# One transformer megakernel: the expert layer in steps of two units, a changed fill table, x2 transposes ahead of the bias product

## The chip, the cores and the metric

One core of a Trainium2 chip runs the whole program in one launch. The metric is the device time of that core in microseconds (us), as the median of several executions. Engines: PE is TensorE, DVE is VectorE, ACT is ScalarE, POOL is GpSimd, SP is SyncE (it only issues transfers).

## The reference

Sixteen images and sixteen texts of 128 tokens become sequences of 178 tokens of width 192 (49 image tokens, one class token, the text). Two layers follow. The first is an attention with a masked diagonal. The second is an attention whose logits are z-scored, followed by a layer of four experts of which each token takes two:

```python
h = concat([tokenize(x), txt])
h = h + attention(layernorm(h))                  # 12 heads, the token itself masked out
s = layernorm(h)
logits = gamma * zscore(Q K^T / 4);  a = softmax(logits) V Wo
x2 = layernorm(s + a)
combine = top2(softmax(x2 Wg + bg))              # 4 experts
hid = relu(x2 W1[e] + b1[e])                     # 192 -> 768
y   = hid W2[e] + b2[e]                          # 768 -> 192
h = h + layernorm(x2 + sum_e combine[e] * y[e])
```

## The kernel before

The sixteen sequences are taken in eight pairs. After the tokenizer (until about 166 us) the kernel runs nine rounds, each with up to three pairs in flight: pair a in the first attention, pair b in the second, pair m in the expert layer. `rounds` writes them out: round 0 (a=0), round 1 (a=1, b=0), rounds 2 to 6 (a, b=a-1, m=a-2, and the front of pair a+1), round 7 (a=7, b=6, m=5, no next pair), round 8 (b=7, m=6, no a), and a last round with m=7 alone. Rounds 2 to 6 and the last use the table `FILL`, round 7 `FILL_A7`, round 8 `FILL_B7`.

A round on PE: the gate products of pair b of the round before (L977), then for pair b turning its rows into columns (`pe_turn_in`, L747), query and key projections (L755), value projection (L763), the four products of the z-score (`pe_deviation`, L876 to L899); for pair a the max pass (`pe_max_pass`: logits whose row maximum DVE takes, L790 and L796, DVE L1271), the rows of maxima (L823), the exp pass (logits again, ACT's exp at L1031, the product with the values at L849); then max pass and rows for b; the output of a (`pe_out`: L858, L864, L763), the exp pass of b, the output of b; then turning in, query and key of the next pair (L747, L755); then what is left of the expert layer (`moe.rest()`), the transposes of x2 of pair b (L964), and the value projection of the next pair. The gate products of b wait for DVE's `x2T_lo` (L1389).

The expert layer of pair m is 24 units (4 experts, six blocks of 128 hidden columns). Unit u has a first product F(u), 5 matmuls of 370 columns (L644), ACT's relu into one of two `hid` buffers (L679), and a second product S(u), 3 matmuls that the profile shows as 6 instructions (L666). After each sixth S, DVE adds the expert's share to `acc` (`expert`, L694). At the end comb is transposed (call it C, L635), ACT copies it (L683), PE multiplies it with the bias b2 (`bias`, B, L654), and DVE adds that (L703, L705).

These units are cut into 50 steps, and every engine takes its part of the same steps at the same named points of its own program. The table says how many steps stand at each point:

```python
def point(self, name, u=None):
    self.steps(self.fill[name] if u is None else self.fill[name][u])
```

Step 2u is F(u); step 2u+1 is S(u-1); step 48 is C and S(23); step 49 is B. The order is fixed by the program, and each engine runs its own in order; waits between engines are semaphores. The steps on DVE matter for the order there: the share of an expert stands at the point in which its sixth S falls. DVE's order around a round's end is: output of b, the chain that makes x2 (to L1378), the scaling for the next pair b (L1135), the point "next query", the splits of the next pair's queries and keys into three bf16 terms (`splits`, L1142 to L1145, eight operations), `moe.rest()`, then `x2T_lo`.

## Time and profile before

| | |
|---|---|
| three executions | 1286.83, 1287.30, 1294.15 us (median 1287.3) |
| profiled execution | 1291.78 us |
| its span, first to last instruction | 1290.0 us |
| mean granted TensorE clock | 0.884 of 2.4 GHz |
| busy | PE 1095.4 us (85%), PE weight loads 802.2, DVE 682.1 (53%), ACT 399.7 (31%), POOL 54.1 |

The profiled execution is 1.8 us longer than its span and 4.5 us above the median. By round it runs from 391 to 512 us (round 2), about 119.6 us each for rounds 3 to 6, to 1110 (round 7), to 1225 (round 8), and to 1290 (the last).

### The profile page before, as it was taken

To read this page: it belongs to the slowest core of one execution; us is meant where nothing else is said; L and a number is where in the kernel's file an instruction comes from. 1 tells how busy PE (TensorE), PEld (TensorE's weight loads), DVE (VectorE), ACT (ScalarE), POOL (GpSimd) and SP (SyncE) were. 2 spreads that over 40 slices of the span, in tenths; PEclk is the share of its full clock that TensorE was granted. 3 is DMA by queue.
4 is the path that set the end of the run, shared out by engine and by line. 5 is a ranking of instruction groups with operands and counts; after the bars stand their busy time and mean duration, and the time that the engine had idled before them with its cause. 6 is when DMAs were issued, how large, how long until landed. Compare 5 with 4: busy or idle time off the path is not lost.

```text
span 1290.0 us, 18666 instructions
## 1 busy us (share of the span) xinstructions
PE 1095.4 (85%) x7404; PEld 802.2 (62%) x7404; DVE 682.1 (53%) x1874; ACT 399.7 (31%) x905; POOL 54.1 (4%) x89
## 2 busy tenths in 40 slices
PE   7898645587779999999999999999999999985896
PEld 4343323354448668857776786678578667773795
DVE  1467685345454466654763674655557652632332
ACT  1222221212232433334323434333343234221321
POOL 6011100000000000000000000000000000000000
PEclk9898855755779989989998999899999989895988
DMA  8000051053005202320422043014204220022000
GB/s 296 0 1 0 16 152 26 7 97 61 11 7 119 49 8 56 78 43 9 84 51 44 8 105 66 13 34 100 44 8 82 51 43 2 1 64 29 1 10 8
DMA packets 38478, 60.74 MB, mean 47 GB/s; under 512 B 5060, under 2 KB 30264, under 8 KB 38072
## 3 DMA queue, kind: packets, MB, share of 16 engines
q1 hardware_dynamic: 36112, 56.84, 20.5%
q10 hardware_dynamic: 2280, 2.72, 0.7%
q8 instruction: 58, 0.95, 0.3%
q14 instruction: 28, 0.23, 0.1%
HBM read 42.76 MB, written 16.34 MB: 46 GB/s over the span
## 4 chain that ended last, share of the span: by engine, by line
PE 63%; DVE 13%; ACT 4%; issue 3%; DMA 3%; SPq 1%; POOL 0%; DVEq 0%; ACTq 0%; POOLq 0%
PE PS L666 14%; PE PS L644 11%; PE PS L755 7%; DVE mx L1271 6%; PE PS L849 5%; PE PS L763 5%; PE PS L790 5%; PE PS L796 3%; PE PS L805 2%; PE PS L858 2%; DMA qst<-mrows 1%; PE PS L887 1%; PE PS L977 1%; ACT probs L1031 1%; SPq L1471 1%
## 5 line engine op out<-in xcount | busy, mean ns | idle before, releaser
L666 PE MATMUL PS<-w,hid 128*128 128x192 f32 x1152 | 232.1, 339 | 3.0 <-DVE acc L694 1.8
L679 ACT ACTIVATE hid<-PS,b 128x370 f32<-128x370 f32 x192 | 109.1, 569 | 331.6 <-PE PS L644 329.8
L666 PEld LDWEIGHTS PS<-w,hid 128*128 128x128 f32 x1152 | 199.0, 197 | 12.8 <-issue 4.7
L1271 DVE TENSOR_REDUCE mx<-PS 128x2 f32<-128x356 f32 x288 | 129.8, 522 | 131.6 <-PE PS L790 103.5
L1031 ACT ACTIVATE probs<-PS 128x356 f32<-128x356 f32 x288 | 112.9, 484 | 35.6 <-PE PS L790 20.6
L790 PE MATMUL PS<-kst,qst 96*128 96x178 bf16 x384 | 71.5, 284 | 31.7 <-DMA kst<-scr_k 13.6
L644 PE MATMUL PS<-x2T_hi,w_hi 128*128 128x370 f32 x192 | 91.7, 478 | 0.0
L755 PE MATMUL PS<-xT,w_at 96*96 96x370 f32 x192 | 76.0, 546 | 8.9 <-ACT q L998 5.2
L805 PE MATMUL PS<-masks,ident_bf 128*128 128x256 bf16 (+1 forms) x288 | 79.9, 278 | 0.0
L790 PE MATMUL PS<-qst,kst 99*128 99x178 bf16 x384 | 58.0, 254 | 21.7 <-DMA qst<-mrows 17.5
L849 PE MATMUL PS<-probs,va 128*17 128x178 f32 x1536 | 70.8, 327 | 6.4 <-ACT probs L1031 6.4
L790 PEld LDWEIGHTS PS<-kst,qst 96*128 96x128 bf16 x384 | 27.2, 106 | 66.0 <-DVE mx L1271 30.7
L1292 DVE RECIPROCAL rs<-PS 128x36 f32<-128x36 f32 x16 | 6.1, 383 | 114.4 <-PE PS L858 114.4
L644 PE MATMUL PS<-x2T_hi,w_lo 128*128 128x370 f32 x192 | 66.2, 345 | 0.0
L644 PE MATMUL PS<-x2T_lo,w_hi 128*128 128x370 f32 x192 | 66.1, 344 | 0.0
L644 PE MATMUL PS<-x2T_hi,w_rest 128*128 128x370 f32 x192 | 66.1, 344 | 0.0
L644 PE MATMUL PS<-x2T_lo,w_rest 128*128 128x370 f32 x192 | 65.6, 342 | 0.0
L755 PEld LDWEIGHTS PS<-xT,w_at 96*96 96x96 f32 x192 | 33.4, 182 | 41.9 <-ACT q L998 8.9
L790 PEld LDWEIGHTS PS<-qst,kst 99*128 99x128 bf16 x384 | 28.7, 101 | 46.9 <-issue 30.8
L849 PEld LDWEIGHTS PS<-probs,va 128*17 128x17 f32 x1536 | 41.0, 99 | 24.4 <-ACT probs L1031 9.3
L694 DVE SCALAR_TENSOR_TENSOR acc<-PS,comb,acc 128x192 f32<-128x192 f32 x72 | 25.5, 410 | 54.3 <-PE PS L666 54.2
L377 DVE SCALAR_TENSOR_TENSOR dwo<-pad_l,chan,dwo 96x441 f32<-96x441 f32 x48 | 38.0, 793 | 27.9 <-ACT cw L301 26.4
(222 smaller groups left out, 1724.4 us busy)
## 6 DMA issues: line engine op xcount, KB each, us to landing
qst<-scr_q SPq DMA_DIRECT2D x96, 144.0 KB, 4.8
scr_q<-qs SPq DMA_DIRECT2D x16, 432.0 KB, 3.3
scr_k<-ks SPq DMA_DIRECT2D x16, 432.0 KB, 4.7
kst<-scr_k SPq DMA_DIRECT2D x16, 432.0 KB, 5.0
kst<-scr_k SPq DMA_DIRECT2D x16, 288.0 KB, 5.9
cols<-in_x_cols SPq DMA_DIRECT2D x6, 392.0 KB, 8.2
w<-in_w SPq DMA_DIRECT2D x1, 2304.0 KB, 25.2
kst<-scr_k SPq DMA_DIRECT2D x16, 144.0 KB, 6.3
```

What stands on the lines that cost most here:

```text
L377: ch.link(nc.vector.scalar_tensor_tensor(out=out, in0=image_rows(PAD_OF[r][:, 0, :], tap_offset(t), n), scalar=col(C_DW + 18 * r + t), in1 ...
L644: ins = nc.tensor.matmul(PS[:, 4 + u % 2, 0:XN], w[:, f], x[:, plane, 0:XN], start=(k == 0), stop=(k == 4))
L666: ins = nc.tensor.matmul(tile_psum((6, 7), i), hid[u % 2][:, 128 * i:128 * i + 128], w2[:, u, :], start=(j == 0 and i != 1), stop=(j == FT ...
L679: nc.scalar.activation(hid[u % 2][:, 0:XN], PS[:, 4 + u % 2, 0:XN], ACT.Relu, bias=b1[:, u:u + 1]).then_inc(S["h_ready"], 1)
L755: ins = nc.tensor.matmul(PS[0:HC, FRONT[s][m], 0:XN], w_at[:, w, k, HC * m:HC * m + HC], x[:, k, 0:XN], start=(k == 0), stop=(k == 1))
L763: ins = nc.tensor.matmul(tile_psum(banks, i), tile_cols(x, k, i), w_at[:, w, k, :], start=(k == 0), stop=(k == 1))
L790: ins = nc.tensor.matmul(PS[:, bank, T * b:T * b + T], still[0:rows_, h, TP * b:TP * b + NTXT], move[0:rows_, h, TP * b:TP * b + T], start ...
L796: ins = nc.tensor.matmul(PS[64 * b:64 * b + 64, 2, T * g:T * g + T], still[0:rows_, 2 * u + g, TP * b + NTXT:TP * b + TP], move[0:rows_, 2 ...
L805: ins = nc.tensor.matmul(own, ident_bf[:], m.rearrange("p (b j) -> p b j", b=2), start=False, stop=True, skip_group_check=True)
L849: ins = nc.tensor.matmul(PS[32 * q:32 * q + VW, 3, T * b:T * b + T], va[s][:, 2 * i + b, h, :], pr, start=(i == 0), stop=(i == 1), skip_gr ...
L1031: nc.scalar.activation(probs[:, u % PROB_UNITS, bank, :], PS[:, bank, 0:T2], ACT.Exp)\
L1271: nc.vector.tensor_reduce(out, PS[:, g, 0:T2].rearrange("p (b j) -> p b j", b=2), AX.X, ALU.max)\
```

## The change

A step now holds two units: step 2d is F(2d), F(2d+1), step 2d+1 is S(2d), S(2d+1), step 24 is C alone, step 25 is B; 26 steps in all. The three tables are rewritten in these steps. The point ("rows", 1) is now passed also by a round without pair a (in the table of round 8 it holds 3). At the end of a round PE runs what is left of the steps except B, then the x2 transposes, then B. Work and buffers are the same.

What stands at which point in rounds 2 to 6, before and after:

| point | before | after |
|---|---|---|
| start | F0 F1 S0 | F0 F1 S0 S1 |
| norm | F2 | F2 F3 |
| query | S1 F3 S2 F4 | S2 S3 F4 F5 |
| key | S3 F5 S4 | S4 S5 F6 F7 |
| kc | F6 S5 | S6 S7 |
| g | F7 S6 | F8 F9 |
| u | F8 | S8 S9 |
| ss | S7 F9 | F10 F11 |
| split 0 | S8 F10 | S10 S11 |
| rows 0 | S9 F11 S10 F12 | F12 F13 S12 S13 |
| split 1 | S11 F13 | F14 F15 |
| turn 0 | S12 F14 | S14 S15 |
| back 0 | S13 | F16 F17 |
| rows 1 | F15 | |
| exp 1 (six units) | S14, -, F16, S15, -, F17 S16 | -, S16 S17, -, F18 F19, -, S18 S19 |
| turn 1 | F18 S17 | F20 F21 |
| back 1 | F19 | |
| next norm | S18 F20 S19 | S20 S21 F22 F23 |
| next query | F21 S20 | S22 S23 |
| before the x2 transposes | F22 S21 F23 S22 C S23 B | C |
| after them | | B |

In round 8 before, start to "u" hold F0 to F7 and S0 to S6, "ss" holds F8 to F14 and S7 to S13; after, "query" and "key" hold F0 to F3, S0, S1, "ss" holds S2 to S11 and F4 to F13, "split 1" S12 S13, "rows 1" F14 F15 S14 S15 F16 F17.

```diff
-MOE_STEPS = 2 * UNITS + 2
+DUOS = UNITS // 2
+MOE_STEPS = 2 * DUOS + 2
...
 FILL = {
-    "start": 4, "norm": 1, "query": 4, "key": 3, "value": 0, "kc": 2, "g": 2, "u": 1, "ss": 2,
-    ("max", 0): (0, 0, 0, 0, 0, 0), ("split", 0): 2, ("rows", 0): 4, ("exp", 0): (0, 0, 0, 0, 0, 0), ("out", 0): 0,
-    ("max", 1): (0, 0, 0, 0, 0, 0), ("split", 1): 2, ("turn", 0): 2, ("back", 0): 1, ("rows", 1): 1,
-    ("exp", 1): (1, 0, 1, 1, 0, 2), ("out", 1): 0, ("turn", 1): 2, ("back", 1): 1, "next turn": 0, "next norm": 3,
-    "next query": 2,
+    "start": 2, "norm": 1, "query": 2, "key": 2, "value": 0, "kc": 1, "g": 1, "u": 1, "ss": 1,
+    ("max", 0): (0, 0, 0, 0, 0, 0), ("split", 0): 1, ("rows", 0): 2, ("exp", 0): (0, 0, 0, 0, 0, 0), ("out", 0): 0,
+    ("max", 1): (0, 0, 0, 0, 0, 0), ("split", 1): 1, ("turn", 0): 1, ("back", 0): 1, ("rows", 1): 0,
+    ("exp", 1): (0, 1, 0, 1, 0, 1), ("out", 1): 0, ("turn", 1): 1, ("back", 1): 0, "next turn": 0, "next norm": 2,
+    "next query": 1,
 }
...
 FILL_A7 = {
-    "start": 4, "norm": 4, "query": 4, "key": 0, "value": 0, "kc": 1, "g": 2, "u": 1, "ss": 2,
-    ("max", 0): (0, 1, 0, 0, 0, 0), ("split", 0): 2, ("rows", 0): 4, ("exp", 0): (1, 0, 0, 0, 0, 0), ("out", 0): 0,
-    ("max", 1): (0, 0, 1, 0, 0, 0), ("split", 1): 2, ("turn", 0): 2, ("back", 0): 1, ("rows", 1): 0,
-    ("exp", 1): (1, 2, 0, 0, 0, 1), ("out", 1): 1, ("turn", 1): 2, ("back", 1): 0, "next turn": 0, "next norm": 4,
-    "next query": 2,
+    "start": 2, "norm": 2, "query": 2, "key": 0, "value": 0, "kc": 1, "g": 1, "u": 0, "ss": 1,
+    ("max", 0): (0, 0, 0, 0, 0, 0), ("split", 0): 1, ("rows", 0): 2, ("exp", 0): (0, 0, 0, 0, 0, 0), ("out", 0): 0,
+    ("max", 1): (0, 0, 0, 0, 0, 0), ("split", 1): 1, ("turn", 0): 1, ("back", 0): 1, ("rows", 1): 0,
+    ("exp", 1): (0, 1, 0, 0, 0, 1), ("out", 1): 0, ("turn", 1): 1, ("back", 1): 0, "next turn": 0, "next norm": 0,
+    "next query": 0,
 }
 FILL_B7 = {
-    "start": 4, "norm": 1, "query": 3, "key": 4, "value": 0, "kc": 2, "g": 0, "u": 2, "ss": 14,
-    ("max", 0): (0, 0, 0, 1, 1, 0), ("split", 0): 0, ("rows", 0): 0, ("exp", 0): (0, 0, 0, 0, 0, 0), ("out", 0): 1,
-    ("max", 1): (0, 0, 0, 0, 0, 0), ("split", 1): 1, ("turn", 0): 1, ("back", 0): 2, ("rows", 1): 4,
-    ("exp", 1): (1, 2, 0, 0, 0, 2), ("out", 1): 1, ("turn", 1): 2, ("back", 1): 0, "next turn": 0, "next norm": 3,
-    "next query": 2,
+    "start": 0, "norm": 0, "query": 2, "key": 1, "value": 0, "kc": 0, "g": 0, "u": 0, "ss": 10,
+    ("max", 0): (0, 0, 0, 0, 0, 0), ("split", 0): 0, ("rows", 0): 0, ("exp", 0): (0, 0, 0, 0, 0, 0), ("out", 0): 0,
+    ("max", 1): (0, 0, 0, 0, 0, 0), ("split", 1): 1, ("turn", 0): 0, ("back", 0): 0, ("rows", 1): 3,
+    ("exp", 1): (0, 1, 0, 0, 0, 1), ("out", 1): 0, ("turn", 1): 1, ("back", 1): 0, "next turn": 0, "next norm": 0,
+    "next query": 0,
 }
...
+            def step(self, d, odd):
                 pe, m = self.eng, self.m
...
+                if odd and d == DUOS:
                     self.bias()
                 elif odd:
...
+                    for u in range(2 * d, 2 * d + 2):
+                        self.second(u)
+                elif d == DUOS:
                     pe.wait_ge(S["comb_ready"], at(m, 1, 1))
...
                     ins.then_inc(S["ct_psum"], 1)
-                    self.second(UNITS - 1)
...
+                    for u in range(2 * d, 2 * d + 2):
+                        self.first(u)
...
-            moe.rest()
+            moe.steps(MOE_STEPS - 1 - moe.done)
             if b is not None:
...
                 ins.then_inc(S["x2T_psum"], 1)
+            moe.rest()
             if nxt is not None:
                 pe_value(pe, 0, nxt)
```

## Rows read from the trace of the kernel before

**Rows 1.** Page, the chain that ended last, by engine.

```profile
PE 63%; DVE 13%; ACT 4%; issue 3%; DMA 3%; SPq 1%; POOL 0%; DVEq 0%; ACTq 0%; POOLq 0%
```

**Rows 2.** Windows: stretch, length, busy by engine (instructions), granted clock, DMA share, GB/s.

```profile
632.10:751.70 119.60, 113.26 (x875) 87.41 (x876) 71.55 (x212) 44.46 (x105) 2.22 (x4) 0.97 0.24 50
...
1110.00:1225.00 115.00, 89.62 (x584) 73.56 (x584) 44.43 (x128) 31.59 (x69) 1.33 (x2) 0.83 0.14 27
1225.00:1290.00 65.00, 51.26 (x285) 49.72 (x285) 20.06 (x74) 14.33 (x26) 0.67 (x1) 0.87 0.03 9
```

**Rows 3.** Timeline of PE, round 4: start, length, line, operands, count [idle before].

```profile
634.19 0.34 PE L644 MATMUL PS<-x2T_lo,w_rest 128*128 128x370 f32 x1
634.36 0.34 PE L644 MATMUL PS<-x2T_hi,w_hi 128*128 128x370 f32 x1
...
642.37 1.14 PE L666 MATMUL PS<-w,hid 128*128 128x192 f32 x6
643.21 0.47 PE L644 MATMUL PS<-x2T_hi,w_hi 128*128 128x370 f32 x1
643.52 0.34 PE L644 MATMUL PS<-x2T_hi,w_lo 128*128 128x370 f32 x1
```

**Rows 4.** PE's waits in round 4: total, times, longest.

```profile
PE PS L823 <- DVE mpart L1280: 1.0, 1, 1.0
```

**Rows 5.** Timeline of PE, round 4, output of a and exp pass of b.

```profile
706.52 2.22 PE L763 MATMUL PS<-w_at,oT 96*128 96x192 f32 x12
708.44 0.46 PE L644 MATMUL PS<-x2T_hi,w_hi 128*128 128x370 f32 x1
...
709.65 0.48 PE L790 MATMUL PS<-qst,kst 99*128 99x178 bf16 x4
...
724.29 1.17 PE L858 MATMUL PS<-ident,osb 128*128 128x128 f32 x9 [0.73 <-ACT osb L1042]
```

**Rows 6.** Timeline of PE, round 4, output of b.

```profile
727.70 0.42 PE L644 MATMUL PS<-x2T_hi,w_hi 128*128 128x370 f32 x1
...
728.83 2.22 PE L763 MATMUL PS<-w_at,oT 96*128 96x192 f32 x12
```

**Rows 7.** Timeline of DVE, end of round 4.

```profile
738.55 0.76 DVE L1378 TENSOR_TENSOR x_wide<-x_wide,rows 128x576 f32<-128x576 f32 x1
...
740.10 0.52 DVE L1142 CAST qs<-q 96x712 bf16<-96x712 f32 x1
...
745.14 0.90 DVE L1145 TENSOR_TENSOR ks<-rem,ks 96x712 bf16<-96x712 f32 x1
746.50 1.07 DVE L694 SCALAR_TENSOR_TENSOR acc<-PS,comb,acc 128x192 f32<-128x192 f32 x3 [0.47 <-PE PS L666]
...
750.61 0.96 DVE L1389 TENSOR_TENSOR x2T_lo<-PS,x2T_hi 128x768 fp32r<-128x768 f32 x1 [0.82 <-ACT x2T_hi L1114]
```

**Rows 8.** Start of round 2: PE's gates, then the window behind them.

```profile
390.94 0.24 PE L977 MATMUL PS<-gate_a,x2T_hi 128*128 128x8 f32 x1 [1.79 <-DVE x2T_lo L1389]
```

```profile
392.30:398.00 5.70, 5.70 (x29) 5.65 (x28) 2.57 (x14) 1.86 (x4) 0.00 (x0) 0.70 1.02 156
```

**Rows 9.** Windows, start of round 8: the gates, then the first products.

```profile
1110.00:1112.60 2.60, 2.48 (x12) 2.51 (x12) 0.00 (x0) 0.00 (x0) 0.00 (x0) 0.50 0.00 0
1112.60:1117.30 4.70, 4.70 (x18) 4.66 (x19) 2.58 (x14) 1.35 (x3) 0.00 (x0) 0.57 0.01 3
```

**Rows 10.** Timeline of DVE, second max pass of round 7, behind F(13).

```profile
1056.95 4.01 DVE L1271 TENSOR_REDUCE mx<-PS 128x2 f32<-128x356 f32 x9 [1.07 <-PE PS L790]
```

**Rows 11.** Round 8: DVE's share of expert 1, then PE's first logits.

```profile
1152.74 1.07 DVE L694 SCALAR_TENSOR_TENSOR acc<-PS,comb,acc 128x192 f32<-128x192 f32 x3 [12.64 <-PE PS L666]
```

```profile
1170.02 0.75 PE L790 MATMUL PS<-kst,qst 96*128 96x178 bf16 x4 [13.03 <-issue]
```

**Rows 12.** Timeline of PE, last round, around S(5) and S(6).

```profile
1240.79 1.14 PE L666 MATMUL PS<-w,hid 128*128 128x192 f32 x6
...
1243.26 1.21 PE L666 MATMUL PS<-w,hid 128*128 128x192 f32 x6 [0.49 <-DVE acc L694]
```

More of the change, by code:

```diff
@@ L670, in build, with step @@
         class MoeAct(Moe):
-            def step(self, u, odd):
+            def step(self, d, odd):
                 act, m = self.eng, self.m
-                if not odd and u < UNITS:
+                if odd:
+                    return
+                if d == DUOS:
+                    act.wait_ge(S["ct_psum"], at(m, 1, 1))
+                    nc.scalar.copy(combT[:, 0:XN], PS[0:E, 4, 0:XN]).then_inc(S["ct_ready"], 1)
+                    return
+                for u in range(2 * d, 2 * d + 2):
                     act.wait_ge(S["h_psum"], at(m, UNITS, u + 1))
@@ L706, in bias, with step @@
                 dve.wait_ge(S["y_used"], at(m, E + 1, E + 1))
-            def step(self, u, odd):
-                if u == UNITS and odd:
+            def step(self, d, odd):
+                if d == DUOS and odd:
                     self.bias()
-                elif u and u % FT == 0 and (odd or u == UNITS):
-                    self.expert(u // FT - 1)
+                elif odd and (2 * d + 2) % FT == 0:
+                    self.expert((2 * d + 2) // FT - 1)
             def finish(self):
@@ L727, in build, with steps @@
         class NoMoe:
+            done = 0
             def rest(self):
+                pass
+            def steps(self, n):
                 pass
@@ L943, in pe_round @@
                 pe_out(pe, 0, a, moe)
-                moe.point(("rows", 1))
+            moe.point(("rows", 1))
+            if a is not None:
                 pe.wait_ge(S["pr_read", 0], at(a, 1, 1))
@@ L1097, in act_round @@
                 act_out(act, 0, a, moe)
-                moe.point(("rows", 1))
+            moe.point(("rows", 1))
             if b is not None:
@@ L1360, in dve_round @@
                 norm1 = dve_norm1(dve, a)
-                moe.point(("rows", 1))
+            moe.point(("rows", 1))
             if b is not None:
```

26 lines of the change are left out of this document (10 added, 16 removed).

## The prediction

> **What bounds the kernel now.** I read the page's chain first: PE carries 63% of it and DVE 13% [rows 1]. Then the stretches by round: rounds 2 to 6 repeat in 119.6 us with PE busy 113.3, so most of a round is PE's own work, but round 8 and the last round leave PE idle 25 and 14 us [rows 2]. Busy PE is not the whole story, so I walked round 4 in PE's timeline, point by point, asking at each whether the next instruction came when PE was free or when something else was ready. Three kinds of places come out.
>
> PE-bound places: start, norm, query, key, kc, g, u, ss, turn 0, back 0, turn 1, next norm. Work put there costs its length.
>
> Pinned places: in the max passes DVE's maxima set the pace; after split 0 PE waits 1.0 us for DVE's split maxima, after rows 0 it waits likewise for the transfer of the maxima rows [rows 4]. Work put there is free up to the wait. So is it at rows 1: the output projection starts at 706.52, PE is free for F(15) at 708.44, and the exp pass may start at 709.65, when DVE has read the projection [rows 5]. And at back 1: F(19) starts at 727.70, the projection at 728.83, when ACT has copied its operand [rows 6].
>
> The end of a round: PE's gates come right behind DVE's x2T_lo, which ends at 751.57 [rows 7]. There DVE waited twice for PE (0.47 us ahead of the last expert's share, and for the bias product), so PE leads and DVE follows.
>
> **What a step costs.** A first product next to another starts its matmuls every 0.17 us, 0.86 in all for five (634.19 to 634.36). A second product is 0.84 us (642.37 to 643.21). The matmul that follows one takes 0.31 until the next, not 0.17: leaving a run of second products costs 0.14 us [rows 3]. Pairs halve these exits, 24 to 12 a round. Two second products in a row do not occur in the trace. The exit cost inside such a pair lies between 0 (as inside two first products) and 0.14 (as in leaving them); I take 0, since the same instruction follows.
>
> The Trainium skill (TensorE: Matmul & The Clock Gate, Part 3, the mechanism) says that weight loads overlap matmuls in flight only when they use other row groups. All these products use all rows, so by that rule an operand's load would be paid wherever the step stands, and pairing would save nothing. The 0.17 against 0.31 of [rows 3] speaks for a difference; it is kept as a rival.
>
> **Rounds 2 to 6, from the gates to the output projection of b (96.7 us before).** After minus before, in us:
> - start: S(1) more, +0.84. norm: one F more, less a wait of 0.19 for ACT that it hides, +0.67. query: same work, one exit less, -0.14. key: F more, exit less, +0.72. kc, g, u, ss together: one S and no F more (0.84), two exits less and a wait of 0.30 hidden, +0.30.
> - split 0, rows 0, split 1: the same number of products in front of the same waits, 0.
> - turn 0: -0.03. back 0: F F for S, +0.75.
> - rows 1 and back 1: nothing stands there now. Both are pinned, so they give nothing back: PE idles some 1.0 and 0.9 us more, behind DVE's read and ACT's copy. The two first products that stood there are paid elsewhere.
> - exp pass of b: 14.64 us before (709.65 to 724.29) with 3 S and 2 F in it [rows 5]; after, 4 S and 2 F in three pairs. I laid it out bank by bank (exp ready 0.88 us after its logits start, a pair of S 1.92 with entry and exit, a pair of F 1.90, values 1.33 each): 15.3. +0.67, bounds +0.3 and +1.1.
> - turn 1: two F for F S, -0.11.
>
> Sum +3.67: two S and two F have moved here from the end of the round (3.4), and what pairing saves is eaten by the two empty points.
>
> **Rounds 2 to 6, from that projection to the next gates (22.9 us before).** PE has 3.4 us less to do, and B no longer stands ahead of the x2 transposes. But the last expert's share now falls at "next query" on DVE, ahead of the eight split operations; queued behind it are the splits, the bias sum and x2T_lo, and PE's gates wait for that. DVE's own chain: projection start 728.83 to x2 done 739.31, 10.48; scaling 0.8; share 1.1; splits 740.10 to 746.04, 5.94; bias 0.9; x2T_lo 1.0; gates 0.1 behind it [rows 6, 7]. Sum 20.3. PE would be ready after 18.1 (2.05 and 0.66 for L763 and L747, 3.53 and 1.84 for the pairs, 2.49 each for query and key, 1.1 for C and the x2 transposes, 1.0 waiting for ACT's copy of C behind the key copies, 0.95 for B, 1.95 for the values). DVE ends last: 22.9 to 20.3 is -2.5. What is late next is x2T_lo, and PE idles 2.2 us ahead of the gates.
>
> So a round of this kind is +1.1 us, five are +5.7. The share of expert 1 now stands on DVE ahead of the query split of b (1.1 us later). Its transfers had about 1.9 us to spare before max pass 1, so I cost it at nothing; without that cover it is up to 1.1 a round.
>
> **The clock.** The idle time ahead of the gates has a price. Round 2 began just so: 1.79 us of idle before the gates, and behind them the clock was granted at 0.70 on average over 5.7 us, so it stood at 1.2 GHz for a good part of them, with PE fully busy [rows 8]. 0.30 of 5.7 us is 1.7 us lost. Round 4 had no such idle, and its clock was 0.97 as a whole [rows 2]. After, five starts follow 2.2 us of idle, and 1.0 us a little earlier. I take a fall in three of five, +5.1; bounds 0 and 8.5.
>
> **Round 7.** It loses the steps inside the passes. DVE's gap of 1.07 us in the second max pass shows what F(13) cost there [rows 10]; with F(9) in the first (0.5) and S(11) in the exp pass of a (0.9) it is -2.7 together, some of it at the lower clock. Back 0 +0.75, start and the rest +0.4, the end +0.2 (two F more there, but B, transposes and copies now overlap). -1.4.
>
> **Round 8.** The query split waits on DVE for the share of expert 1, which waits for S(11); from there to max pass 1 are 17.3 us (1152.74 to 1170.02) in which PE idles 13 [rows 11]. The new table still puts S(11) in "ss", ahead of the split. Emptying start, norm, kc and u exposes the waits that they hid, and S(11) comes at about the same time (+0.4), with fewer products done. "rows 1" then fills the transfer of the maxima rows, where PE idled, but overruns it: output projection +1.1. The end of the round is shorter by 2.5: two S fewer, and B, transposes and copies overlap. -1.0, bounds -3 and +3.
>
> **The last round.** It is PE alone. Eleven exits less, -1.5. Three times S of the next expert waited for DVE's share: 2.47 us between starts against 1.84 (0.84 + 0.14 + 0.86) [rows 3, 12]; two first products now stand there and cover it, -2.2. C moves into the last such wait, -0.5. -4.2.
>
> **Sum.** +5.7 +5.1 -1.4 -1.0 -4.2 = +4.2 us on the profiled execution, 1291.8 to 1296.0. That execution lies 4.5 above the median; the same +4.2 on 1287.3 gives **1291.5**. 1% of this kernel (12.9 us) is about what a measurement can tell from no change.
>
> **Rivals.**
> - The clock holds: no fall at any start. For it: round 4 idles ahead of B too (the share's gap of 0.47 on DVE and the share itself), and kept 0.97 [rows 2, 7]. Against: the start of round 2 [rows 8]. Price: -0.9 in all, 1286.4. The Trainium skill (the same page, Why this matters for your kernels) counts only longer idle gaps as a cause of a fall; by that rule this is the case.
> - The clock falls deeper (the slower side): as at round 8's start, where the gates ran at 0.50 for 2.6 us and the first products at 0.57 for 4.7: 1.3 and 2.0, 3.3 us lost [rows 9]. Five times that is +15.6 in all: 1303. It decides if the clock is already at 1.2 GHz when the gates begin; four such falls of five pass 1%.
> - DVE does not end last at the round's end: then PE's 18.1 counts, 2.2 us less five times, and no fall: -12 in all, 1275. Against it: the sum of rows 7 has no slack in it.
> - Pairing saves nothing: seven exits a round stay in PE-bound places, eleven in the last round, about 7 us: 1298.
>
> **How the numbers follow.** Forecast 0.45 (1284 to 1298 by its own bounds), clock holds 0.22, clock deeper 0.11, DVE not last 0.14, no saving 0.08. Faster than 1274.4 takes the DVE case and a little more, 0.13; slower than 1300.2 takes most of the deeper fall and a tail of the others, 0.13; 0.74 is within 1%. The range 1276 to 1300 leaves out about 0.2.
>
> **What would show it.** Rounds 2 to 6 at 120 to 123 us between gates. PE idle about 1.2 us ahead of the exp pass of b and 1.1 ahead of the output projection of b; about 2 us ahead of the gates with DVE x2T_lo as releaser, and DVE with no gap between its splits and x2T_lo. A window behind the gates at 0.7 to 1.0. In the last round no wait of L666 for DVE, S(0) to B about 4 us shorter. Round 8: the first logits still 17 us behind expert 1's share. The prediction is wrong if the gates of rounds 3 to 7 come without idle, or if a round is under 119.

## The result and the profile after

The changed kernel takes 1325.5 us (median of 4 runs, 1319.7 to 1330.9), the kernel before 1290.7 on the same chip (1286.8 to 1294.2): ratio 1.027, 95% interval 1.023 to 1.031. It is 2.7% slower. The forecast was 1291.5, with a range up to 1300. The profiled execution took 1321.5 with a span of 1319.7.

The chain of waits, by engine, to be set beside [rows 1]:

```profile
PE 57%; DVE 19%; issue 4%; ACT 4%; DMA 2%; SPq 1%; POOL 0%; DVEq 0%; POOLq 0%; ACTq 0%
```

DVE has taken part of PE's share of the chain: PE waits more often. Windows by round (rounds 4, 8 and the last), columns as in [rows 2]:

```profile
640.50:767.30 126.80, 116.91 (x876) 91.61 (x876) 71.54 (x212) 44.49 (x105) 2.56 (x4) 0.93 0.24 47
...
1138.90:1256.70 117.80, 92.26 (x584) 73.33 (x584) 45.03 (x128) 31.44 (x69) 2.10 (x2) 0.83 0.13 26
1256.70:1319.70 63.00, 51.02 (x285) 49.07 (x285) 20.04 (x74) 14.35 (x26) 0.67 (x1) 0.88 0.03 9
```

Round 4 took 119.6 us with PE busy 113.3 at a clock of 0.97. Now it takes 126.8, PE busy 116.9 at 0.93. The count of PE's records is the same but for one (876 and 875). More busy time for the same work is the first sign of the clock.

Lengths from gates to gates, in us:

| round | 2 | 3 | 4 | 5 | 6 | 7 | 8 | last | from round 2's gates to the end |
|---|---|---|---|---|---|---|---|---|---|
| before | 121.4 | 119.8 | 119.6 | 119.5 | 119.5 | 119.4 | 114.8 | 65.0 | 899.1 |
| after | 125.8 | 125.8 | 126.8 | 126.6 | 125.9 | 119.1 | 117.8 | 63.0 | 930.8 |

Rounds 2 to 6 lose 31.1, round 8 loses 2.9, the last gains 2.0, round 7 gains 0.2. The last column is what I use below. The part ahead of round 2's gates runs the same instructions in all kernels here, but took between 385.3 and 399.9 us in the profiled executions. A difference of medians carries that spread, the last column doesn't. But the last column is one execution of each kernel and has a spread of its own: r8_table (below) runs rounds 2 to 6 with the instructions of the changed kernel and took 3.3 us less for them, with single rounds up to 3.1 apart. Three kernels whose rounds 2 to 6 are alike and lose little to the clock (x2t_only, x2t_last_pairs, pairs_end) agree there within 1.1.

**The starts.** Windows of PE alone: one ahead of round 5's gates, then the starts of rounds 3, 4, 5, 6 and 7 (window, length, PE busy, granted clock, DMA share, GB/s):

```profile
765.20:767.30 2.10, 0.98 (x6) 0.55 0.29 79
516.70:521.00 4.30, 4.30 (x16) 0.50 1.00 167
640.40:646.00 5.60, 5.54 (x28) 0.70 1.03 150
767.30:772.00 4.70, 4.70 (x19) 0.50 1.03 156
893.90:899.00 5.10, 5.10 (x20) 0.50 1.05 133
1019.80:1025.00 5.20, 5.20 (x26) 0.67 1.02 143
```

Rounds 3, 5 and 6 begin at 1.2 GHz throughout. Rounds 4 and 7 begin at 2.4 and fall some 2 us later. All five starts are hit. Timeline of PE, round 5's gates, and timeline of DVE, end of round 3 (last share, splits, bias sum, x2T_lo):

```profile
767.29 0.34 PE L992 MATMUL PS<-gate_a,x2T_hi 128*128 128x8 f32 x1 [1.12 <-DVE x2T_lo L1404]
767.49 0.35 PE L992 MATMUL PS<-gate_a,x2T_lo 128*128 128x8 f32 x1
```

```profile
631.55 1.06 DVE L702 SCALAR_TENSOR_TENSOR acc<-PS,comb,acc 128x192 f32<-128x192 f32 x3
632.64 0.53 DVE L1157 CAST qs<-q 96x712 bf16<-96x712 f32 x1
...
638.50 0.55 DVE L711 TENSOR_TENSOR acc<-PS,acc 128x384 f32<-128x384 f32 x1
...
639.35 0.96 DVE L1404 TENSOR_TENSOR x2T_lo<-PS,x2T_hi 128x768 fp32r<-128x768 f32 x1
```

DVE works without a gap from the share to x2T_lo, as forecast. PE's gates wait for it. They start every 0.20 us in round 5, every 0.10 to 0.11 where the clock is at 2.4.

**Pairs of second products.** Timeline of PE, round 4:

```profile
651.97 2.12 PE L671 MATMUL PS<-w,hid 128*128 128x192 f32 x12
653.78 0.47 PE L649 MATMUL PS<-x2T_hi,w_hi 128*128 128x370 f32 x1
654.09 0.33 PE L649 MATMUL PS<-x2T_hi,w_lo 128*128 128x370 f32 x1
```

Two second products are 1.81 us (651.97 to 653.78), not 2 x 0.84 = 1.68, and the first product behind the pair still takes its 0.31. The timeline of PE's weight loads over the same stretch shows why:

```profile
651.97 1.82 PEld L671 LDWEIGHTS PS<-w,hid 128*128 128x128 f32 x11
653.76 0.19 PEld L649 LDWEIGHTS PS<-x2T_hi,w_hi 128*128 128x128 f32 x1
653.92 0.19 PEld L649 LDWEIGHTS PS<-x2T_hi,w_lo 128*128 128x128 f32 x1
654.09 0.19 PEld L649 LDWEIGHTS PS<-x2T_lo,w_hi 128*128 128x128 f32 x1
```

The loads come every 0.16 to 0.17 us, inside the pair (0.163 for each of eleven) and across its end (0.16, 0.17). No time is added at either place. What is out of step is one start: the matmul behind the last record of a second product is stamped 0.03 us after that record's start, and the next one 0.30 later (0.33 together, as 0.16 and 0.17 would be). So the 0.84 is five steps of 0.163 and this 0.03, and the 1.81 eleven steps and the same 0.03. A second product costs six steps, 0.98, wherever it stands. In the last round the two take 1.88 (as in x2t_last_pairs below), because the first weight load of the pair waits some 0.07 for ACT's relu.

**The query stacks.** Timelines of DVE, the SP queue and PE, rounds 4 and 5. Expert 1's share stands ahead of the query's first operation (L1272); the queue stores the split query, then issues the stacks; the second max pass (L803, kst and qst) waits:

```profile
686.56 1.06 DVE L702 SCALAR_TENSOR_TENSOR acc<-PS,comb,acc 128x192 f32<-128x192 f32 x3
687.65 0.96 DVE L1272 SCALAR_TENSOR_TENSOR q<-q,chan,rem 96x712 f32<-96x712 f32 x1
```

```profile
691.67 0.31 SPq L1476 DMA_DIRECT2D scr_q<-qs  x1
696.04 2.64 SPq L1480 DMA_DIRECT2D qst<-scr_q  x6
...
833.67 0.75 PE L803 MATMUL PS<-kst,qst 96*128 96x178 bf16 x4 [1.53 <-issue]
```

The stacks are issued 4.4 us behind the store (3.3 before). From the exp pass of a to the second max pass PE took 11.25 us before, and takes 13.1, 12.8 and 12.1 in rounds 4, 5 and 6.

**The output of a.** Two rounds, 2 and 4, lose another 2.0 us each later on, between the first transposes of a's output and its back turn: 4.97 us where rounds 3, 5 and 6 take 2.99 and the kernel before 2.88. PE window of that stretch in round 4:

```profile
716.94:721.91 4.97, 4.97 (x22) 0.59 0.04 9
```

In these two rounds the low clock that begins in the second max pass lasts into this stretch.

**Round 8.** Timelines of DVE and PE, to be set beside [rows 11]:

```profile
1188.17 1.07 DVE L702 SCALAR_TENSOR_TENSOR acc<-PS,comb,acc 128x192 f32<-128x192 f32 x3 [10.12 <-PE PS L671]
```

```profile
1204.85 0.75 PE L803 MATMUL PS<-kst,qst 96*128 96x178 bf16 x4 [15.05 <-issue]
```

The share starts 49.3 us behind the gates, where it started 42.6 behind them. The chain behind it is no longer than before (16.7 us from the share to the logits, 17.3 before).

### The profile page after: what moved, and what is told of

It is laid out like the page before. It is cut to its first block, busy times and chain, and to the rows that moved or that the text cites. A ratio compares the mean times of both kernels' runs of the same rounds, so it can differ in the third digit from the quotient of the medians.

```text
span 1319.7 us, 18662 instructions
## 1 busy us (share of the span) xinstructions
PE 1109.9 (84%) x7404; PEld 817.5 (62%) x7404; DVE 682.5 (52%) x1874; ACT 399.4 (30%) x905; POOL 56.2 (4%) x89
## 3 DMA queue, kind: packets, MB, share of 16 engines
q1 hardware_dynamic: 36112, 56.84, 20.1%
## 4 chain that ended last, share of the span: by engine, by line
PE 57%; DVE 19%; issue 4%; ACT 4%; DMA 2%; SPq 1%; POOL 0%; DVEq 0%; POOLq 0%; ACTq 0%
PE PS L649 12%; PE PS L671 12%; DVE mx L1286 5%; PE PS L803 5%; PE PS L862 5%; PE PS L768 4%; PE PS L776 4%; PE PS L809 3%; PE PS L818 2%; PE PS L871 2%; PE PS L992 1%; PE PS L900 1%; DMA qst<-mrows 1%; ACT probs L1046 1%; SPq L1486 1%
## 5 line engine op out<-in xcount | busy, mean ns | idle before, releaser
L671 PE MATMUL PS<-w,hid 128*128 128x192 f32 x1152 | 217.0, 340 | 0.2
L803 PE MATMUL PS<-kst,qst 96*128 96x178 bf16 x384 | 71.6, 284 | 38.2 <-issue 19.2
L649 PE MATMUL PS<-x2T_hi,w_hi 128*128 128x370 f32 x192 | 81.0, 422 | 0.6 <-ACT mrows L1037 0.6
L803 PE MATMUL PS<-qst,kst 99*128 99x178 bf16 x384 | 57.8, 252 | 23.1 <-DMA qst<-mrows 13.9
L803 PEld LDWEIGHTS PS<-kst,qst 96*128 96x128 bf16 x384 | 27.0, 106 | 72.9 <-issue 36.7
L649 PE MATMUL PS<-x2T_lo,w_rest 128*128 128x370 f32 x192 | 68.4, 356 | 0.0
L803 PEld LDWEIGHTS PS<-qst,kst 99*128 99x128 bf16 x384 | 27.5, 101 | 48.7 <-issue 26.1
```

The lines of the kernel that those rows point to most:

```text
L649: ins = nc.tensor.matmul(PS[:, 4 + u % 2, 0:XN], w[:, f], x[:, plane, 0:XN], start=(k == 0), stop=(k == 4))
L671: ins = nc.tensor.matmul(tile_psum((6, 7), i), hid[u % 2][:, 128 * i:128 * i + 128], w2[:, u, :], start=(j == 0 and i != 1), stop=(j == FT ...
L803: ins = nc.tensor.matmul(PS[:, bank, T * b:T * b + T], still[0:rows_, h, TP * b:TP * b + NTXT], move[0:rows_, h, TP * b:TP * b + T], start ...
```

## The experiments

All ran beside the kernel before, whose medians there lay between 1290.3 and 1292.7. "End" is the time from round 2's gates to the end of the profiled execution.

| kernel | median us | ratio to before, 95% | end |
|---|---|---|---|
| before | 1290.7 | | 899.1 |
| after | 1325.5 | 1.023 to 1.031 | 930.8 |
| keep_clock | 1316.0 | 1.015 to 1.022 | 923.5 |
| keep_clock_2 | 1316.6 | 1.015 to 1.023 | 914.8 |
| before_gap | 1319.3 | 1.020 to 1.028 | 925.2 |
| x2t_only | 1285.4 | 0.993 to 0.998 | 892.4 |
| pairs_only | 1327.4 | 1.024 to 1.031 | 935.1 |
| query_first | 1338.8 | 1.032 to 1.039 | 947.4 |
| query_first_2 | 1341.3 | 1.033 to 1.040 | 947.6 |
| shift | 1317.2 | 1.018 to 1.027 | 923.6 |
| pairs_mended | 1327.0 | 1.024 to 1.032 | 928.2 |
| pairs_mended_clock | 1307.2 | 1.008 to 1.015 | 914.6 |
| r8_table | 1316.5 | 1.017 to 1.024 | 921.6 |
| keep_all | 1300.1 | 1.002 to 1.009 | 904.4 |
| x2t_last_pairs | 1285.6 | 0.993 to 0.998 | 891.0 |
| pairs_end | 1283.5 | 0.992 to 0.998 | 890.6 |

### The clock

**keep_clock.** Nothing of the computation changes; ten products are added that nobody reads.

```
+ if m is not None and nxt is not None:
+     for _ in range(10):
+         nc.tensor.matmul(PS[:, 5, 0:T2], ident_bf[:], masks[:, 0:T2], start=True, stop=True, ...)
  pe.wait_ge(S["x2T_lo"], at(b, 1, 1))
```

> The changed kernel, with ten products of 370 bf16 columns into PSUM bank 5, which nobody reads, put on PE behind the values of the next pair and ahead of the wait for x2T_lo, in rounds 2 to 6 (1.6 us of work at 2.4 GHz in an idle stretch of 1.7 to 2.1). Nothing of the computation changes. Theory (the idle stretch ahead of the gates lets the clock fall): the gates of rounds 3 to 7 come at the same offset from the projection of b (20.1 us), with steps of 0.11 us and not 0.21, and gates to turn falls from 6.7 (rounds 4, 7) and 9.0 (rounds 3, 5, 6) to about 5.0: 3 x 4.0 + 2 x 1.6 = 15 us less, about 1310. Rival 1 (the clock falls at the start whatever PE did, because of what ran in the tail as a whole or in the round before): no change, 1325. Rival 2 (the added products run at the low clock themselves, 0.31 us each, and end behind x2T_lo): the gates come 1 to 1.5 us later in each round, up to 1333.

1316.0, 9 less than the changed kernel. PE windows and two rows of its timeline, round 5's start:

```profile
762.00:764.00 2.00, 2.00 (x13) 1.00 0.80 210
764.00:765.50 1.50, 1.50 (x7) 0.53 0.04 14
765.50:767.60 2.10, 2.10 (x9) 0.52 0.98 191
767.70:769.00 1.30, 1.30 (x14) 1.00 1.00 138
...
765.14 2.85 PE L989 MATMUL PS<-masks,ident_bf 128*128 128x356 bf16 x10
767.70 0.29 PE L996 MATMUL PS<-gate_a,x2T_hi 128*128 128x8 f32 x1
```

Both sides were partly right. The gates run at 2.4 GHz and gates to turn is 5.2 us in all five starts. But the clock had fallen at 764, ahead of the added products. They ran at 0.26 us each and outlasted x2T_lo: the gates came 21.6 us behind the projection of b, 1.5 later. The only idle time in the 15 us before 764 was the wait ahead of B, 0.82 us at 761.4.

**keep_clock_2.** Eight products there, and five between the x2 transposes and the bias product.

> The changed kernel again with products that nobody reads, now in two places of rounds 2 to 6: five between the x2 transposes and the bias product, where PE waited 0.82 us for ACT, and eight ahead of the wait for x2T_lo. In keep_clock the clock had fallen before the ten products began (0.53 from 764.0 on, some 2.6 us behind the wait ahead of B), they ran at 0.26 us each and ended 1.4 us behind x2T_lo. Theory (the waits of PE in the round's tail, the one ahead of B included, let the clock fall): with both filled the clock stays at 1.0, the gates come at 20.1 us from the projection of b, gates to turn is 5.2 us at most in rounds 3 to 7: 1.4 x 5 less than keep_clock, about 1309, 16 less than the changed kernel. Rival (the fall comes from idle time further back, ahead of the projection of b and of its exp pass): the clock still falls in the tail, the products run at half clock and end late: 1316 or more.

PE windows at the start of round 5 and at the exp pass of b in round 4; and the timeline of PE at round 5's start:

```profile
769.00:774.20 5.20, 5.19 (x35) 1.00 1.09 144
...
726.90:732.70 5.80, 4.89 (x26) 0.71 0.13 34
```

```profile
767.51 1.37 PE L993 MATMUL PS<-masks,ident_bf 128*128 128x356 bf16 x8
769.01 0.27 PE L1000 MATMUL PS<-gate_a,x2T_hi 128*128 128x8 f32 x1
```

All five starts are at 2.4 GHz (gates to turn 5.2 us in each), and the gates come as early as in the changed kernel (20.0 us behind the projection of b). From round 2's gates to the end it is 914.8 against 930.8: 16.0 less, as the theory said. The median moved by 9 only. This profile has 399.9 us ahead of round 2, the longest such part of all. The 16.0 is not the starts alone: from the gates to the turn of rounds 3 to 7 it is 14.2 less, and the rest is a sum of things that went both ways. Rounds 2 and 4 no longer lose the 2.0 us each in the output of a, but round 7 loses 1.8 there; the waits for the query stacks are 2.4 less; and the clock falls in the exp pass of b of rounds 4 and 6, behind the empty point "rows 1", for 1.5 and 1.7 us (second window), which the changed kernel doesn't show.

**before_gap.** The other way round: the kernel before, two steps taken from the end of the round.

```
-    "start": 4,  ...  "next norm": 3,
+    "start": 6,  ...  "next norm": 1,
```

> The kernel before with two steps (a first and a second product) taken from next norm and put at the start of the round, in single steps and nothing else: PE has 1.84 us less to do at the round's end and stands idle ahead of the bias product instead, 2.5 us where it was 1.16. Theory (idle time at the round's end costs the clock, whatever the size of the steps): the clock falls behind it in most of rounds 2 to 7, 2 to 4 us each time, and the pair costs its 1.84 at the start while the end gives back 0.4: 15 to 25 us more, 1305 to 1317. Rival (the clock held in the kernel before for another reason than the small idle time, the single steps for example): 1.4 x 5, about 1299.

1319.3, but mostly not by the clock. PE's waits in round 4, and PE windows at the ends of rounds 3, 2 and 4:

```profile
PE PS L654 <- DVE acc L694: 2.2, 1, 2.2
PE PS L864 <- DVE x_wide L1293: 1.9, 1, 1.9
```

```profile
637.60:645.20 7.60, 6.64 (x22) 0.55 0.85 143
511.80:519.20 7.40, 6.91 (x25) 0.54 0.92 129
764.40:775.00 10.60, 9.99 (x63) 1.00 0.78 149
```

The wait ahead of B is 2.2 us in every such round. The clock fell with it at the ends of rounds 2 and 3 and held at the end of round 4, and at that of round 5 as well; round 7's start was slow again (7.8 us to turn, 4.2 before). Round 5 lost 3.7 us with the clock at 2.4 GHz at its start: 1.8 for the two steps there and 1.9 ahead of the back turn of b, where PE now waits for DVE; the end of the round gave 0.5 back. So the same idle time was followed by a fall at two ends and not at two others. What decides in each case is not settled by these runs. And moving two steps from the end to the start cost all of them there, and gave 0.5 back.

### The parts of the change

**x2t_only.** The x2 transposes ahead of the bias product, in the kernel before, and nothing else.

> The kernel before, in single steps with its own tables, with the x2 transposes put ahead of the bias product: that part of the change alone. Theory (B and its wait for the last share leave the chain to the gates, while PE has no new idle): 0.5 to 1.5 us less in each of eight rounds, 1279 to 1287. Rival (DVE's chain from its last share to x2T_lo has the bias sum in it as before, so the gates come no earlier): no change, 1290. Rival 2 (PE now waits for DVE ahead of the gates and the clock falls, as in the changed kernel): gates at the low clock, 5 to 15 us more.

1285.4, 0.5% less than before. Timelines of PE and DVE at the end of round 4:

```profile
745.97 1.24 PE L654 MATMUL PS<-b,hid 4*128 4x192 f32 x6 [0.51 <-DVE acc L694]
...
748.17 0.96 DVE L1395 TENSOR_TENSOR x2T_lo<-PS,x2T_hi 128x768 fp32r<-128x768 f32 x1
```

From the last share to the gates it is 4.4 us, 5.2 before: the 0.82 that x2T_lo waited for ACT's copy [rows 7] is gone, and PE's wait ahead of B fell from 1.16 to 0.51. Rounds 3 to 6 gain 0.2 to 0.7, round 2 1.3, round 7 1.9, round 8 0.9, the last 1.0.

**pairs_only.** The changed kernel with the transposes put back behind the bias product.

> The changed kernel with the x2 transposes put back behind the bias product: steps of two and the new tables alone. Theory: the wait for the last share and B (0.95 us) are on the chain again, so the gates come 0.5 to 1.5 us later in each round, and the idle time ahead of the gates (2.1 us) shrinks by what PE does later; the clock still falls, since PE waits in all as long: about 1332. Rival (the order of B makes the idle stretch ahead of the gates, and without it the clock holds): starts as short as 5 us, 1310 to 1315.

1327.4, not to be told from the changed kernel. Rounds 2 to 6 lie between 123.2 and 129.5, by where the clock fell. The gates come 20.1 us behind the projection of b, as in the changed kernel, where 0.5 to 1.5 more was expected. The whole loss is in the pairs and their tables.

**x2t_last_pairs.** x2t_only, with PE alone in pairs in the last round (lines of the edit joined).

```
+ if b is None and nxt is None and m is not None:
+     moe.second(1)
+     for u in range(2, UNITS, 2):
+         moe.step(u, 0); moe.step(u + 1, 0); moe.second(u)
+         if u + 2 < UNITS: moe.second(u + 1)
+     moe.step(UNITS, 0); moe.done = MOE_STEPS - 1
```

> x2t_only (single steps, x2 transposes ahead of the bias product) with PE alone in pairs in the last round: two first products, two second products. Theory (the matmul behind a second product takes 0.13 more whether it is a first or a second one, so a pair saves no exit, 3.67 us for a pair against 2 x 1.84): only the three waits for DVE's shares go, 3 x 0.49 to 0.63, with up to 0.07 more per pair where a second product waits for ACT: 1 to 2 us less than x2t_only, 1284. Rival, the prediction's term (a pair saves 0.14 for each exit that it spares, eleven of them, besides the waits): 3.5 us less, 1282.

The last round is 62.7 us against 64.1: 1.4 less, the size of the three waits for DVE's shares (3 x 0.49) that are gone. Timeline of PE:

```profile
1236.53 2.18 PE L666 MATMUL PS<-w,hid 128*128 128x192 f32 x12
1238.41 0.47 PE L644 MATMUL PS<-x2T_hi,w_hi 128*128 128x370 f32 x1
...
1240.24 2.19 PE L666 MATMUL PS<-w,hid 128*128 128x192 f32 x12
```

A pair of each is 3.71 us (1236.53 to 1240.24), two single steps of each are 3.67; the difference is mostly the wait for ACT's relu. Pairing saves nothing.

### The query's split and the shares

**query_first.** DVE's order alone.

```
-                moe.point(("split", 0))
             if b is not None:
                 query(a)
             if a is not None:
+                moe.point(("split", 0))
                 moe.point(("rows", 0))
```

> The changed kernel, with DVE's split of the query of b ahead of its share of expert 1, not behind it; nothing else moves. Theory (the stacks of the query are late because DVE split it 1.1 us later): max pass b starts right behind exp pass a in rounds 4 to 6, where it waited 1.9, 1.6 and 0.9 us, and the last stack transfer is issued 1.1 us earlier: 4 us less, about 1321. Rival (the transfers are late for another reason, such as what else is in the queue, so that 1.1 us earlier in the split gives only part): 1 to 2 us less. Rival 2 (the share, now 5 us later, makes the first second product of expert 2 wait in the fill of rows 0): each round 1 to 2 us longer, 1333. Round 8 should gain as well, since its query split stands behind the share in the same way: 1 us.

1338.8, 13 more. From the exp pass of a to the second max pass it is 11.25 us in rounds 3, 4 and 5, so the wait is gone there; rounds 2 and 6 take 11.9 and 12.1. But PE's waits in round 5 have a new first row:

```profile
PE PS L671 <- DVE acc L702: 2.6, 1, 2.6
```

Rival 2 holds: in rows 0 PE needs expert 2's accumulator, and DVE's share is late by the split.

**query_first_2.** query_first, with "rows", 0 at 1 and "split", 1 at 2: that pair of second products moved behind the max pass.

> query_first (DVE's query split ahead of its share of expert 1) with the second products 12 and 13, which wait for that share, taken from rows 0 to split 1 of rounds 2 to 6, where a share that is 6 us later is long done. Theory (the share ahead of the split costs the wait ahead of max pass b, and query_first lost only by the new wait of 2.6 us in rows 0): max pass b starts 11.25 us behind exp pass a in all rounds, rows 0 still takes 4.9 (the transfer of the maxima rows sets it), split 1 has a pair more for 0.9 us of wait: from the gates of round 2 to the end 924 to 928 where the changed kernel has 930.8 and query_first 947.4. Rival (the pair in split 1 costs its whole 1.8, and emptying rows 0 brings another fall of the clock): 932 or more.

1341.3. The wait for the stacks is gone in rounds 3, 5 and 6 (11.25), not in rounds 2 and 4 (13.9 and 12.6). PE's wait in rows 0 is 2.6 us again, now for the transfer of the maxima rows:

```profile
PE PS L803 <- DMA qst<-mrows: 2.6, 1, 2.6
```

Both halves of the rival hold. From the second max pass to the maxima rows it is 12.4 to 13.4 us, 10.7 in the changed kernel: the pair that was moved there costs its whole 1.8 and more. And the clock falls in the exp pass of b of all five rounds, which takes 16.9 to 17.1 us instead of 15.4. As to the cause of the wait for the stacks: the kernels with the share ahead of the split lose 1.6 to 6.2 us to it in rounds 2 to 6 together (4.4 in the changed kernel), shift and pairs_mended below, with the share behind it, 0.3 and 0. So the order matters; but query_first and query_first_2, which have the share behind the split as well, still lose 1.5 and 4.0, and what delays the stacks in them is open.

**shift** and **pairs_mended.** shift has start at 1 and next query at 2, so that the sequence runs one pair later. pairs_mended has start at 1 and next query at 1; its last pair of second products and its last share come behind the splits. It has r8_table's table as well.

> The changed kernel with the whole sequence of pairs one pair later: one at the start instead of two, two at the end of the round instead of one (rounds 2 to 6). The second products 10 and 11 then stand in rows 0, and DVE's share of expert 1 behind its split of the query, without the wait that query_first made (there PE needed expert 2's accumulator in rows 0; here first at split 1). Theory: start 1.8 less at full clock, tail at most 0.5 longer, because DVE was last there by 2; the wait ahead of max pass b gone (4.4 in three rounds); some of the falls of the clock gone with the idle time: 3 to 5 us less a round, 1300 to 1310. Rival (the pair of second products in the tail makes the last share late, which DVE needs ahead of the splits, so the end of the round is longer by 1.8): 1320 to 1325.

> The changed kernel with pairs, one pair fewer at the start of rounds 2 to 6, the last pair of second products in the round's end behind next query (so DVE's last share stands behind its splits), and the table of r8_table for round 8. Theory (the loss is in four places that a table can move: the clock behind idle time, the wait for the query stacks, the share ahead of the splits, round 8): shift lost 2.4 us in the round's end again, because its last share stood ahead of the splits and waited for PE; without that 1.9 to 2.4 less in each of five rounds than shift, and 5.6 less in round 8: about 1300. Rival (PE has as much to do in the round's end as DVE has, and the share waits for the pair behind the key): 0.5 a round, 1309.

shift gains 8, where I expected 15 to 25. At the end of round 5 DVE's share waits for PE ahead of the splits, and the end is 22.5 us long where it was 20.1, so the rival took back most of it:

```profile
879.26 1.07 DVE L702 SCALAR_TENSOR_TENSOR acc<-PS,comb,acc 128x192 f32<-128x192 f32 x3 [2.31 <-PE PS L671]
```

pairs_mended missed badly: 1327 where 1300 was expected. Timeline of DVE, end of round 5:

```profile
893.47 1.06 DVE L702 SCALAR_TENSOR_TENSOR acc<-PS,comb,acc 128x192 f32<-128x192 f32 x3
895.93 0.56 DVE L711 TENSOR_TENSOR acc<-PS,acc 128x384 f32<-128x384 f32 x1 [1.40 <-PE PS L659]
...
896.79 0.96 DVE L1404 TENSOR_TENSOR x2T_lo<-PS,x2T_hi 128x768 fp32r<-128x768 f32 x1
```

With the share behind the splits, share, B and bias sum form one chain, 3.3 us from the share to x2T_lo. In the changed kernel the share is early, B runs beside the splits, and only the bias sum (0.85) is left on that chain. The place of the last share was the good part of the new order. PE also waits 2.5 us ahead of B, and the starts of rounds 3 to 6 take 5.8 to 5.9 us to turn, 3.2 at 2.4 GHz.

**pairs_mended_clock.** pairs_mended with added products in three waits.

> pairs_mended with products that nobody reads in three waits of PE in rounds 2 to 6: five ahead of the exp pass of b (rows 1), five between the x2 transposes and the bias product, eight ahead of the gates. Theory: the clock stays at 1.0 through rounds 3 to 6, so what is left of the loss against the kernel before is what the pairs themselves cost in waits and exits, 0.5 to 1.5 us a round: 1291 to 1298. Rival (what is left in pairs_mended is not clock): no less than pairs_mended; where the products outlast a wait they add up to 0.5 us a round.

1307.2: 20 less than pairs_mended by the medians, 13.6 by the ends. The clock was half of its loss again. Rounds 3 to 6 are still 124 to 125 us, by the chain just shown; the expected 1291 to 1298 rested on that order being good.

### Round 8, and the sum

**r8_table.** The table of the kernel before for round 8, halved.

```
-    "start": 0, "norm": 0, "query": 2, "key": 1, ... "kc": 0, ... "u": 0, "ss": 10, ... ("back", 0): 0, ("rows", 1): 3,
+    "start": 2, "norm": 1, "query": 1, "key": 2, ... "kc": 1, ... "u": 1, "ss": 7,  ... ("back", 0): 1, ("rows", 1): 2,
```

> The changed kernel with another table for round 8: the counts of the kernel before, halved (start 2, norm 1, query 1, key 2, kc 1, u 1, ss 7, split 1 1, back 0 1, rows 1 2), so that the points that the new table emptied are filled again and S(11) comes earlier in ss. Theory (round 8 got slower because S(11), and with it the share and the query split, came 6 us later while PE stood idle in the emptied points): 3 to 6 us less, 1320. Rival (round 8's length is set by the first exp pass and what follows, and the low clock in ss after the idle time): within 1 us of the changed kernel.

Round 8 is 112.2 against 117.8. Timeline of DVE:

```profile
1190.55 1.07 DVE L702 SCALAR_TENSOR_TENSOR acc<-PS,comb,acc 128x192 f32<-128x192 f32 x3 [13.68 <-PE PS L671]
```

The share starts 43.9 us behind the gates, 5.4 earlier than in the changed kernel, and the round is 5.6 shorter. The median is 9.0 lower and the end 9.2. Of the 9.2, 3.3 lie in rounds 2 to 6, whose instructions are those of the changed kernel, so they are not owed to the table.

**keep_all.** keep_clock_2, five added products ahead of the exp pass of b, and r8_table's table.

> keep_clock_2 with five more products that nobody reads, in the wait of PE ahead of the exp pass of b (rows 1), and with the table of r8_table for round 8: the clock's loss and round 8's removed together, the pairs and their order in rounds 2 to 7 as in the changed kernel. Counted from the gates of round 2 to the end (the stretch ahead of round 2 differs by up to 14 us between runs whatever the kernel), before is 899.1, the changed kernel 930.8, keep_clock_2 914.8. Theory (the three losses add up: clock 16 in five rounds and round 7, a further 1.5 in the exp passes of b of rounds 2, 4 and 6, where the clock fell in keep_clock_2 as well, 5.6 in round 8, and what is left, some 6 us, is order and exits): 904 to 906. Rival (the falls only move on: with the wait of rows 1 filled another follows elsewhere, or the products there delay the exp pass): 909 or more.

904.4, in the middle of what was expected, and the median is 1300.1. PE windows of rounds 5 and 8:

```profile
763.70:885.90 122.20, 115.44 (x893) 0.97 0.24 49
1125.60:1234.10 108.50, 87.46 (x584) 0.88 0.14 28
```

The sum agrees by a different split. Rounds 2 to 7 are only 0.5 less than in keep_clock_2: the falls in the exp pass of b are gone, and the 1.9 us in the output of a are back in rounds 2 and 4, so in part the falls did move on, as the rival said. Round 8 is 11.0 less than there, more than the 5.6 that the table gave r8_table; its mean clock is 0.88, in r8_table 0.85.

**pairs_end.** x2t_only in single steps for rounds 2 to 7, pairs with r8_table's table in round 8, pairs in the last round.

> x2t_only (single steps, x2 transposes ahead of the bias product, tables of the kernel before) with pairs in rounds 8 and the last alone: round 8 with the table of pairs_mended, in which it took 108.9 us against 114.0 in x2t_only, and the last round in pairs, 62.4 against 64.0. Theory (pairs pay where they spare waits at expert boundaries and fill long idle stretches, and cost where a round's small waits are full already): rounds 2 to 7 as in x2t_only, 5 us less in round 8 and 1.5 in the last: 1279. Rival (round 8 was short there because round 7 in pairs handed it an earlier split of the key or a higher clock): round 8 at 112 or more and 1283 to 1285.

1283.5. Round 8 is 111.9 (x2t_only 114.0), the last 63.4 (64.1): 2.7 in these two, not 6.5, and 1.8 by the ends. The rival holds for round 8; its 108.9 in pairs_mended came with round 7 in pairs. The interval overlaps that of x2t_only. Both are 0.2 to 0.8% below the kernel before.

## Why the prediction was wrong

The forecast was +4.2 us; between the two profiled executions, from round 2's gates on, it is +31.7 (the medians differ by 34.7). The clock is the largest error (+18.2 measured where +5.1 stood), the query's split and round 8 come next, and pairing saved nothing.

- **The end of the round, -2.5: right.** DVE works from share to x2T_lo without a gap, gates 20.1 us behind the projection (20.3 forecast), -2.7 to -2.8 measured in rounds 2 to 6.
- **The PE-bound places: nearly right.** Where the clock is the same, start is +1.00 (forecast 0.84), norm +0.68 (0.67), query and key +0.77 (0.58), kc to ss +0.64 (0.30), turn 0 and back 0 +0.78 (0.72), the exp pass of b +0.81 (0.67), turn 1 -0.11 (-0.11), and the empty points gave back 0.1. The sum is +4.5 a round where +3.67 was forecast. The misses are mostly one error, the next.
- **"I take 0, since the same instruction follows": wrong.** The "exit cost" of 0.14 is no cost of leaving second products, and the 0.13 inside a pair no cost of staying: both are the sixth step of a second product, which the early start of the next matmul's record hides in the 0.84 and shows again in the 0.31. With 0.98 for a second product and 0.86 for a first, any order of them costs the same, and there was nothing to halve. So the fourth rival's outcome (no saving) is the true one; x2t_last_pairs shows it. The Trainium skill (TensorE: Matmul & The Clock Gate, Part 3, the mechanism) says that weight loads overlap running matmuls only in other row groups. This trace doesn't agree: loads of all 128 rows, 0.19 us each, come every 0.16 to 0.17 us beside matmuls of all 128 rows, so they do overlap, and the outcome came about for another reason than that rule.
- **The clock, +5.1 with bounds 0 and 8.5: the step that failed most.** "A fall in three of five" starts at 1.7 us each was five of five. Against the same stretch in keep_clock_2 they cost 1.5 in rounds 4 and 7 and 3.7 to 3.8 in rounds 3, 5 and 6, 14.2 together. That is near the 16.5 of the second rival (3.3 five times), partly by luck: its condition ("already at 1.2 GHz when the gates begin") held in three of five, and those cost more than its 3.3. Over the whole of rounds 2 to the last the added products took off 16.0 in one profiled execution and 9 by the medians. I had taken the size from the one mild start of [rows 8] and left falls elsewhere out; those in the output of a of rounds 2 and 4 cost 4.0 more. I asked what idle time was added ahead of the gates, and not how often PE idles in the 20 us before them: 0.9 ahead of the projection, 0.8 ahead of B, 0.8 to 1.4 ahead of the gates. The same page of the Trainium skill (Why this matters for your kernels) asks only that longer gaps be avoided; the starts of rounds 3 to 7 show that this is not enough. Its Part 1 (A second HAM failure mode) says that short idles between groups of matmuls can make the clock swing too; the trace agrees with that.
- **The cover of the query's split, 0: wrong.** The text named a cover of 1.9 us and a price of 1.1 a round without it. In round 4 the stacks were issued 1.1 later behind their store as well, and the wait came to 1.9, 1.6 and 0.9 in rounds 4 to 6, 4.4 us. A term that nobody had: in rounds 2 and 3 the exp pass of a starts 0.8 and 0.4 later behind the rows of maxima, 1.3 together; PE waits there for the transfer of the maxima rows, and why it is late was not tried.
- **Round 8, -1.0: wrong, +2.9.** "S(11) comes at about the same time (+0.4)": it came 6.7 us later, since the emptied points exposed waits of 1.6, 1.0 and 0.9 us and the clock stood lower. The end of the round was right: 14.8 us from the projection of b, 17.3 before, the forecast -2.5.
- **The last round, -4.2: half, -2.0.** The waits for the shares went, the eleven exits (-1.5) did not. The -2.2 for the three waits was too large as well: 2.47 against 1.84 is 0.63 each, 1.9 in all, and the waits themselves are 0.49 each, 1.4 in all.
- **Round 7: -0.2 where -1.4 was forecast,** with its start at the low clock. In keep_clock, where that start is at 2.4 GHz, the round is 117.6, -1.8; so its own terms were nearly right.

The terms add up to the +31.7 of the last column (within 0.1). Here they are beside the forecast's, in us:

| term | forecast | measured |
|---|---|---|
| rounds 2 to 6, work and end of the round | +5.7 | +8.5 |
| clock, starts of rounds 3 to 7 | +5.1 | +14.2 |
| clock, output of a in rounds 2 and 4 | 0 | +4.0 |
| wait for the query stacks | 0 | +4.4 |
| later exp pass of a in rounds 2 and 3 | 0 | +1.3 |
| round 7 without its start | -1.4 | -1.7 |
| round 8 | -1.0 | +2.9 |
| the last round | -4.2 | -2.0 |

As a check, the shortest rounds of keep_all (3, 5 and 6), with no more low clock than the stretch in the second max pass that the kernel before has in every round, take 122.2, 2.7 more than before where +1.1 was forecast: 0.8 of the excess is the wait for the query stacks in rounds 5 and 6, or a later exp pass of a in round 3, and the rest is mostly what pairing was to save.

## What to carry to other kernels

Count PE's idle time over the whole stretch ahead of dense work, and price a fall of the clock at its deepest observed size, not at its mildest: here 1 to 2 us of new idle time cost up to 3.8 us behind it. A cheap test is to fill the wait with products that nobody reads; if the time falls, it was the clock. Before pricing a switch between two kinds of steps by the starts of matmul records, set the weight loads beside them, or add the two neighbouring steps up: what is missing from one can stand in the other. Before grouping steps, look at what DVE work moves with the group: the share's place decided three waits, each of which came back elsewhere when it was cured alone.

## What the runs showed of the hardware

- In keep_clock the clock stood at 1.2 GHz from 764 to 767.6, while PE was fully busy, and came back at 767.7. In the changed kernel, with PE idle in that stretch, it stayed low to 775 (round 5). That the work shortened it is likely, but no run tries it alone.
- 2.2 us of idle ahead of B came with a fall of the clock at the ends of rounds 2 and 3 of before_gap, and with none at those of rounds 4 and 5. The order and the work were the same.
- The part ahead of round 2 took 385.3 to 399.9 us in profiled executions of the same instructions. Its mean clock was 0.74 in keep_clock_2 and r8_table, the two longest, and 0.77 in pairs_mended_clock, the shortest. At full speed the time lost to the low clock would differ by some 14 to 15 us between them (an estimate: length times what is missing from 1.00), about as much as the lengths do (14.6). What sets it was not tried.
- Weight loads of 128 rows and 128 columns (0.19 us each) followed each other every 0.16 to 0.17 us while matmuls of 128 rows and 192 or 370 columns ran (651.97 to 654.09 in the changed kernel). The record of the first matmul behind a second product started only 0.03 us behind the one before it.
